# Attention in a four-layer gated stack: row maxima turned in 32 by 32 blocks on VectorE, contexts divided on GpSimd, one plane of queries, scores six maxima sooner

## Time and profile before

| what | value |
|---|---|
| median of 3 runs | 1188.35 us (1186.31 to 1188.7) |
| profiled execution, its own time | 1189.92 us |
| its span in the profile | 1187.9 us |
| PE busy | 1054.0 us, 89% |
| DVE busy | 783.8 us, 66% |
| ACT busy | 492.1 us, 41% |
| POOL busy | 206.3 us, 17% |
| chain that ended last | PE 60%, DVE 26%, DMA 4%, issue 4%, ACT 3%, POOL 2% |

### The profile page before, as it was taken

One profiled execution on the slowest core, in us unless ns is written; L12 is line 12 of the kernel. 1 busy time (PEld: TensorE's weight loads), 2 busy tenths in 40 slices (PEclk: granted clock), 3 DMA queues, 4 the chain that ended last, 5 costly groups with the idle time before them and its releaser, 6 DMA issues.

```text
span 1187.9 us, 17076 instructions
## 1 busy us (share of the span) xinstructions
PE 1054.0 (89%) x6429; PEld 601.9 (51%) x6429; DVE 783.8 (66%) x1448; ACT 492.1 (41%) x722; POOL 206.3 (17%) x251
## 2 busy tenths in 40 slices
PE   8788958999989878996899998997989997999998
PEld 4233433444434448993344444444778785344445
DVE  5979778888788232555588886824545555688616
ACT  2642430667667501110157674772212211067452
POOL 4556410111110020004111111101300402011000
PEclk9989976899999958998779999999989999689799
DMA  6779701013310516961512231101443440100001
GB/s 209 242 250 332 250 26 61 21 40 121 110 39 12 160 49 227 361 240 51 173 37 47 61 100 29 35 2 36 134 150 106 129 141 2 31 11 12 1 28 35
DMA packets 79571, 121.79 MB, mean 103 GB/s; under 512 B 10125, under 2 KB 53296, under 8 KB 79482
## 3 DMA queue, kind: packets, MB, share of 16 engines
q1 hardware_dynamic: 59782, 79.41, 21.8%
q10 hardware_dynamic: 18932, 39.10, 9.3%
q0 software_dynamic: 768, 2.10, 0.6%
HBM read 92.45 MB, written 27.81 MB: 101 GB/s over the span
## 4 chain that ended last, share of the span: by engine, by line
PE 60%; DVE 26%; DMA 4%; issue 4%; ACT 3%; POOL 2%; ACTq 0%; SPq 0%; DVEq 0%; POOLq 0%
DVE arena L2116 13%; PE bank L1451 11%; PE bank L1411 11%; PE bank L1635 11%; PE st_bank L1563 3%; PE bank L1575 3%; PE st_bank L1436 3%; DMA kparts<-arena 2%; PE bank L1218 2%; PE st_bank L1635 2%; PE st_bank L1368 2%; DVE xn L1746 2%; PE bank L1481 2%; PE bank L1417 1%; DVE bnst L1726 1%
## 5 line engine op out<-in xcount | busy, mean ns | idle before, releaser
L2116 DVE TENSOR_REDUCE arena<-bank 128x1 f32<-128x512 f32 x640 | 400.2, 683 | 66.4 <-PE bank L1411 66.3
L1098 ACT ACTIVATE arena<-st_bank 128x1024 f32<-128x1024 f32 x320 | 316.1, 1022 | 159.9 <-PE st_bank L1436 158.5
L1411 PE MATMUL bank<-g_a 64*128 64x512 f32 x480 | 185.2, 519 | 12.3 <-DVE arena L2116 2.9
L1451 PE MATMUL bank<-arena,vaug 128*9 128x256 f32 (+2 forms) x2560 | 175.1, 392 | 1.7 <-ACT arena L1098 1.7
L1411 PEld LDWEIGHTS bank<-g_a 64*128 64x128 f32 x480 | 75.9, 200 | 122.1 <-DVE arena L2116 83.6
L1635 PE MATMUL bank<-g_a,g_w 128*128 128x512 f32 x512 | 120.3, 396 | 4.3 <-DVE g_w L2320 3.2
L1436 PE MATMUL st_bank<-g_a 64*128 64x512 f32 x480 | 116.9, 443 | 0.0
L1635 PEld LDWEIGHTS bank<-g_a,g_w 128*128 128x128 f32 x512 | 97.7, 192 | 26.1 <-DVE g_w L2320 3.6
L1451 PEld LDWEIGHTS bank<-arena,vaug 128*9 128x9 f32 (+2 forms) x2560 | 56.6, 93 | 80.5 <-issue 42.7
L1411 PE MATMUL bank<-g_x,g_a 64*128 64x512 f32 x160 | 64.2, 531 | 9.5 <-DVE arena L2116 4.3
L1436 PEld LDWEIGHTS st_bank<-g_a 64*128 64x128 f32 x480 | 61.3, 191 | 6.6 <-issue 0.5
(11 more groups left out here) (301 smaller groups left out, 1400.3 us busy)
## 6 DMA issues: line engine op xcount, KB each, us to landing
arena<-in_glu_w SPq DMA_DIRECT2D x39, 512.0 KB, 3.4
arena<-kv_table SPq DMA_DIRECT2D x11, 1024.0 KB, 8.1
ctxT<-in_glu_w ACTq DMA_DIRECT2D x22, 512.0 KB, 6.6
arena<-in_w SPq DMA_DIRECT2D x20, 512.0 KB, 6.0
kparts<-arena ACTq DMA_DIRECT2D x12, 512.0 KB, 5.6
arena<-in_w ACTq DMA_DIRECT2D x12, 512.0 KB, 3.5
xnT<-kv_table SPq DMA_DIRECT2D x5, 1024.0 KB, 7.6
g_a<-kparts SPq DMA_DIRECT2D x24, 192.0 KB
```

What stands on the lines that cost most here:

```text
L1098: act.activation(prob[sl % PROBS], st_bank[sl % 2][:], ACT.Exp, scale=scale).then_inc(exp_ready, 1)
L1411: pe.matmul(bank[TURN_BANKS[place % 3]], Qc[gi % KQ_BUFS][rows, hh, qt * P:(qt + 1) * P], Kc[gi % KQ_BUFS][rows, half * CH:(half + 1) * CH ...
L1451: ins = pe.matmul(bank[7][at:at + dh + 1, 0:D], vaug[l][:, b * KT + 2 * m + i, h0 + hh, :], tiles[:, a], start=(m == 0 and i == 0), stop=( ...
L2116: dve.tensor_reduce(mxh[gi % 2][:, col, hf:hf + 1], bank[TURN_BANKS[place % 3]], AX.X, ALU.max).then_inc(max_red, 1)
```

## The change

- The joined maxima go into a tile of 128 by 32 (the other 24 columns zero), and VectorE turns it in 32 by 32 blocks with one instruction into `mxt`, right behind L2121. Block r holds, on partitions 32r to 32r + 7, the maxima of queries 32r to 32r + 31 of every 128. TensorE's turn and ScalarE's read of it are gone.
- GpSimd makes the two parts from `mxt` over 128 partitions by 32 columns. The sign is moved into the keys' rows, which now hold minus one.
- `shift_load` issues eight DMAs: for each of four blocks and each of two parts, eight partitions of 32 numbers go into both heads' rows.
- `LEAD = HALVES + 8`: a group's sixteenth maximum is eight maxima, four score steps, ahead of its first score.
- `Qc` has one plane of 512 columns for both heads, so it is cleared in half the time; what is loaded is as before.
- A turned context is read by ScalarE right behind its turn, which frees the bank; GpSimd takes the reciprocal (as a power of minus one) and multiplies. The last context of a stage stays with VectorE.
- GpSimd clears the shift rows at score step 1 (`CLEAR_SLOT`) of a group.

```
-LEAD = HALVES + 14
+LEAD = HALVES + 8
+SQ = 32
+SHIFT_DMAS = P // SQ * SHIFT_ROWS
...
-            if u > HALVES and u % HALVES == TURN_LAG:
-                turn("turn", u // HALVES - 1)
-            if u == total:
-                turn("turn", NGROUPS[l] - 1)
+            if u % HALVES == 0:
+                steps.append(("shift", u // HALVES - 1))
     def context(g):
         turn("context", g)
-        later.append((u + NORMAL_AFTER, ("normal", *steps[-1][1:])))
+        steps.append(("normal", *steps[-1][1:]))
...
# SyncE
                 sp.wait_ge(max_lo, gi + 1)
-                for h in range(HG):
+                for r in range(P // SQ):
                     for i in range(SHIFT_ROWS):
-                        row = h * HALF_P + i
-                        sp.dma_start(Qc[gi % KQ_BUFS][row:row + 1, h].bitcast(F32).rearrange("o (q n) -> o q n", n=P),
-                                     shp[gi % 2][i][h * QT:(h + 1) * QT, :].bitcast(F32)).then_inc(shift_ld[gi % KQ_BUFS], 16)
+                        sp.dma_start(Qc[gi % KQ_BUFS][i:i + HALF_P + 1:HALF_P].bitcast(F32).rearrange("h (q r n) -> h q r n", q=QT, n=SQ)[:, :, r],
+                                     shp[gi % 2][i][r * SQ:r * SQ + HG * QT].bitcast(F32)).then_inc(shift_ld[gi % KQ_BUFS], 16)
...
# GpSimd
+                        ch.link(pool.tensor_copy(shp[gi % 2][0], mxt[gi % 2]))
+                        pool.tensor_tensor(shp[gi % 2][1], mxt[gi % 2], shp[gi % 2][0].bitcast(F32), ALU.subtract).then_inc(max_lo, 1)
+                    elif step[0] == "score" and step[2] == CLEAR_SLOT and KQ_BUFS <= step[1] + 3 < NGROUPS[l]:
+                        shift_rows(l, step[1] + 3, shifts, contexts)
+                    elif step[0] == "normal" and step[1] < NGROUPS[l] - 1:
...
+                        ch.link(pool.tensor_tensor(rsum_p, sums[:, :, :, dh], bc(minus_one[:, 0:1].unsqueeze(2), [P, QT, 2 * HG]), ALU.pow))
+                        pool.tensor_tensor(dst, sums[:, :, :, 0:dh], bc(rsum_p.unsqueeze(3), [P, QT, 2 * HG, dh]), ALU.mult).then_inc(norm_ready, 1)
...
# ScalarE
-                        act.activation(shn[gi % 2][0:HG * QT, :], bank[TURN_BANKS[place % 3]][0:HG * QT, 0:P], ACT.Copy, scale=-1.0).then_inc(max_neg, 1)
+                        act.activation(context_sums(l, k), turned[:, :, :, 0:dh + 1], ACT.Copy).then_inc(ctx_read, 1)
...
# TensorE
-                def turn_max(g, place):
-                    pe.transpose(bank[TURN_BANKS[place % 3]][0:HG * QT, 0:P], mxg[gi % 2], ident[:]).then_inc(max_tr, 1)
...
# VectorE
+                def turn_max(g):
+                    gi = GROUP0[l] + g
+                    dve.wait_ge(max_fin, gi + 1)
+                    if gi >= 2:
+                        dve.wait_ge(max_lo, gi - 1)
+                    dve.transpose(mxt[gi % 2], mxg[gi % 2]).then_inc(max_tr, 1)
```

More of the change, by code:

```diff
@@ L457, in build @@
         mxh = [r.take([HG * QT, 2]) for _ in range(2)]
-        mxg = [r.take([HG * QT]) for _ in range(2)]
-        shn = [r.take([P]) for _ in range(2)]
-        shp = [[r.take([P], F32R) for _ in range(SHIFT_ROWS)] for _ in range(2)]
+        mxg = [r.take([SQ]) for _ in range(2)]
+        mxt = [r.take([SQ]) for _ in range(2)]
+        shp = [[r.take([SQ], F32R) for _ in range(SHIFT_ROWS)] for _ in range(2)]
+        ctx_sums = [r.take([QT * 2 * HG * (max(dh for _, dh, _ in ATT.values()) + 1)]) for _ in range(2)]
         pvs = [xnT[:, 1, CH + i * D:CH + (i + 1) * D] for i in range(2)]
-        rsum = r.take([QT, 2 * HG])
+        rsum, rsum_p = r.take([QT, 2 * HG]), r.take([QT, 2 * HG])
         qph = [[r.take([CH], F32R) for _ in range(PARTS)] for _ in range(2)]
@@ L695, in queries_load @@
                 sp.wait_ge(qp_st[k % 2], 16 * PARTS * (k // 2 + 1))
-                load_rows(l, g, [Qc[gi % KQ_BUFS][:, i] for i in range(HG)], qparts[l], slice(b * S, (b + 1) * S))
+                load_rows(l, g, Qc[gi % KQ_BUFS], qparts[l], slice(b * S, (b + 1) * S))
             def shift_load(l, g):
@@ L1084, in attention @@
                         q_store(1, 1, 1)
-                    elif step[0] == "turn":
+                    elif step[0] == "normal" and step[1] < NGROUPS[l] - 1:
                         _, g, place = step
[L1087 to L1090, removed]
-                        act.activation(shn[gi % 2][0:HG * QT, :], bank[TURN_BANKS[place % 3]][0:HG * QT, 0:P], ACT.Copy, scale=-1.0).then_inc(max_neg, 1)
+                        k = (GROUP0[l] + g) // 2
+                        act.wait_ge(pv_tr, k + 1)
+                        if k >= 2:
+                            act.wait_ge(norm_ready, k - 1)
+                        turned = bank[TURN_BANKS[place % 3]].rearrange("p (q h e) -> p q h e", q=QT, h=2 * HG)
+                        act.activation(context_sums(l, k), turned[:, :, :, 0:dh + 1], ACT.Copy).then_inc(ctx_read, 1)
                     elif step[0] == "score":
@@ L1383, in attention @@
                 order = schedule(l)
-                rotation = [step for step in order if step[0] in ("max", "turn", "context", "heads", "out", "hold")]
+                rotation = [step for step in order if step[0] in ("max", "context", "heads", "out", "hold")]
                 def bank_read(place):
@@ L1410, in row_max @@
                         pe.wait_ge(*bank_read(place))
-                    pe.matmul(bank[TURN_BANKS[place % 3]], Qc[gi % KQ_BUFS][rows, hh, qt * P:(qt + 1) * P], Kc[gi % KQ_BUFS][rows, half * CH:(half + 1) * CH],
+                    pe.matmul(bank[TURN_BANKS[place % 3]], Qc[gi % KQ_BUFS][rows, qt * P:(qt + 1) * P], Kc[gi % KQ_BUFS][rows, half * CH:(half + 1) * CH],
                               start=True, stop=True).then_inc(max_mm, 1)
@@ L2105, in attention @@
                 dve.memset(bank[7], 0.0).then_inc(pv_done, 1)
+                for i in range(2):
+                    ins = dve.memset(mxg[i][:, HG * QT:], 0.0)
+                ch.link(ins)
                 if l > 1:
@@ L2140, in attention @@
                         reduce_half(*step[1:])
-                    elif step[0] == "normal":
+                    elif step[0] == "shift":
+                        turn_max(step[1])
+                    elif step[0] == "normal" and step[1] == NGROUPS[l] - 1:
                         normalise_context(*step[1:])
```

92 lines of the change are left out of this document (45 added, 47 removed).

## The result

| | before | after |
|---|---|---|
| median | 1188.53 us (4 runs) | 1249.4 us (4 runs, 1247.17 to 1253.65) |
| profiled execution, its own time | 1189.92 us | 1247.17 us |
| its span | 1187.9 us | 1245.4 us |
| TensorE's mean granted clock | 0.913 | 0.893 |
| three stages, first score's exponential of the first group to that of the last | 186.68, 192.03, 92.61 us | 214.42, 211.62, 104.49 us |

The ratio is 1.051, with a 95% interval of 1.0467 to 1.0554: 61 us slower, where 86 were forecast. A passage is the time from one group's first score to the next one's; there are 37. The last line of the table adds up to 59.2 us more. The spans differ by 57.5. So the whole loss lies between the first scores of consecutive groups, where the prediction put it.

The account below looks back on a forecast made before the run. The kernel was taken as bound by a loop of latencies between PE and VectorE. Waits 76 plus clock 13 less 3 made 86 us on 1189.9, so 1276, or 1274 us on the median's scale; range 1178 to 1305.

Parts of the forecast that it names:

- The wait's price: Ahead of each group's first score: PE waits for the shift's copies, 2.06 us more a group, 76 us over 37 passages.
- The turn and the division: Pairs with a turn and with a context: 2.92 and 3.31 us; 0.66 gained a group, but swallowed by the wait.
- From t0 to SyncE: From the start of the last maximum's pair (t0), through VectorE and GpSimd, to SyncE's first issue: 3.03 us.
- The issues: SyncE's eight shift copies: 0.62 us from one to the next, the eighth issued 4.34 us after the first.
- The rival of cheap issues: Eight copies cost what key loads do, 0.37 us apart; a group 12.15, the kernel 1200 to 1215 us; chance 0.12.
- Landing: From the last copy's issue to PE's score: 1.63 us plus 0.14 pickup, so the path ends at 9.14.
- The rest behind the score: From a group's first score to the next t0, the start of the last maximum's pair: 4.76 us; a group 13.90.
- The clock: Behind the waits: half of the 37 passages pay 0.71 us once for the lower clock, 13 us; bounds 0 and 53.
- The single plane and the middle of a stage: Smaller clears, and heads' turns in mid-stage that fall into a wait: 3 us less in all.
- The start of a stage: Start of each stage: new path ends at 208.07 against the first score's 208.02 before; nothing gained or lost.
- The rival of being in time: Shift path fits under 5.95 to 6.34 us, so groups gain 0.66; 1156 us, up to 1180; chance 0.17.
- The rival of a slow clock in every passage: Each wait is followed by two slow pairs, 1.42 us more; a group 15.3, the kernel 1315 us; chance 0.08.

Follow-up runs that it names:

- the filled kernel: Kernel after, lead of eight, plus five unused identity products on TensorE ahead of each group's first score from the second group on: 1225.01 us, ratio 1.029.
- a lead of 14: Kernel after with only the lead changed, from HALVES + 8 back to HALVES + 14: 1152.95 us, ratio 0.969; 1157.5 us when run again.
- leads of 10 and 12: Kernel after with only the lead changed, to HALVES + 10 and HALVES + 12: 1173.77 us (ratio 0.985) and 1159.75 us (ratio 0.974).
- half of the copies: Kernel after, lead of eight, copying only the shift's high part, four DMAs a group instead of eight: 1159.92 us, ratio 0.973.

## Why the prediction was right in kind and 25 us too high

Its mechanism, PE idle ahead of every group's first score until the last of eight copies lands, is what the trace and the experiments show. Its sizes are less good. The wait's price was forecast at 76 us and is about half of that, the clock's at 13 and is 16 to 30. The two misses have opposite signs, so it is partly luck that the sum is off by only 25. Term by term:

- **The turn and the division.** 2.92 and 3.31 were forecast for the two pairs, and 11.18 a group. With the wait gone they are 2.81 and 3.29, and a group takes 11.18 (22.35 / 2). The turn takes 0.21, where 0.20 was taken. GpSimd's power takes 2.91, where 3 was, and nobody waits for it. But the text put the gain at the division down to its move to GpSimd, and the move is worth nothing that these runs can tell.
- **From t0 to SyncE.** 3.03 forecast, 2.96 measured. VectorE is right to 0.03, and GpSimd needs 0.54 instead of 0.63.
- **The issues.** This is the largest miss. The forecast took 0.62 from one to the next, by L704. The new copy's issue takes 0.495 in the median of 320, and the next begins 0.541 after it ((4.28 - 0.495) / 7). Seven of them are 3.79 instead of 4.34. The rival of cheap issues (0.37) was further off than the forecast. (The loads of keys that it went by are not all of 48 rows, but of 12, 24 and 48.)
- **Landing.** 1.77 with the pickup was taken, from a load of queries out of HBM. It is 1.53 from the last issue to the score, in most passages alike. The 2.0 us of the Trainium skill, page "DMA: Bandwidth & Descriptors", section "Anatomy of one DMA", stand there for DMAs that GpSimd issues, and these are SyncE's. With them the path would be 0.47 longer than the trace has it, so the extra 14 us don't come.
- **The rest behind the score.** 4.76 forecast. With the clock at 1.00 it is 12.87 - 8.28 = 4.59, with the passage of the filled kernel and the path of the kernel after. The whole group is 12.87 against the 13.90 forecast, so the wait costs 1.03 a group over before and not 2.06: 37 x 1.03 = 38 us instead of 76. Of the 1.03 that came less, 0.55 is the issues, 0.24 the landing, 0.17 the rest and 0.07 the way to SyncE. This one term, at twice its size, is more than the whole error. A path of 9.14 was 10% too long, but what counts is its excess over the cover, and that was small.
- **The clock.** 13 us forecast, 0.71 in half the passages. It was 16 to 24, by the experiment with the wait filled. By the passages it is up to 30. Without the three in the middle of the stages, 34 passages are together 37.8 us above 12.87, where the kernel before has 8.1 above its 11.84. The bounds were 0 and 53.
- **The single plane and the middle of a stage.** 3 us less were forecast. The three passages in the middle of the stages are 5.5 us shorter than before (55.15 for 60.65), and at a lead of 14 they are 53.73, so the wait costs almost nothing there. The clears of the whole queries tile take 0.59 us for 0.96, those of the shift rows 0.52 as before; their worth was not tried by itself.
- **The start of a stage.** No gain was forecast. The first score of the first stage is at 207.66 instead of 208.02, 0.36 sooner.

Now 38 + 16 to 24 is 54 to 62, which holds the measured 61. By the passages it is 34 x 1.03 = 35, + 30 - 5.5 = 59, where the stages have 59.2. The rival of being in time needed a path of 5.95 to 6.34, and it is 8.28. The rival of a slow clock in every passage is largely true of the clock: 37.8 us over 34 passages are 1.11 in each, 0.24 of it as before, where the rival took 1.42 and the forecast 0.36. It missed the time by 66 us all the same, as it kept the wait's 76. Nine passages of 13.0 to 13.2 show that the clock does not cost two slow pairs each time.

## What to carry to other kernels

When a step is brought forward in a list written by hand, count its whole path, with the issues of its DMAs one by one, against the work that is left to stand ahead of it. Here 8.3 us stood against 6, and a score step more (2 maxima) was worth 76 us. Small copies are priced by their count: eight issues of 0.54 ate the 1.7 us that the faster turn had given. And a wait in front of TensorE costs more than itself, as the stretch behind it may run at the lower clock; filling the wait with products that nobody uses gave 16 to 24 us back, and is a test that tells the two apart.

## What the runs showed of the hardware

- The issue of a copy from SBUF to SBUF on SyncE took 0.495 us for eight partitions of 32 numbers into two rows, and 0.573 for four partitions of 128 numbers into one row. The prediction drew from the Trainium skill, page "DMA: Bandwidth & Descriptors", section "Why a DMA increments its semaphore by 16 and not by 1", that the new form would be no cheaper. It is 0.078 cheaper. Whether two engines or four run it isn't shown here.
- The landing of these copies, 1.53 us from the issue to the waiting product, grew to 2.2 to 3.8 in 18 waits of three kernels (leads of 10 and 12, half of the copies) in which a 512 KB load of another queue was issued among them or right behind.
- GpSimd's power took 2.91 us on 128 by 16 numbers and 1.04 on 128 by 4: a fixed part of 0.42 and 0.156 for each column, if it is a straight line.
- VectorE's turn of 128 by 32 in 32 by 32 blocks took 0.21 us, little more than joining the maxima (0.17).
